# Reordering the third slot and the router's gate steps in a fused attention and mixture-of-experts kernel

## What the kernel computes

```
x = x + conv_attention(layernorm over channels(x))
    k, q = relu(1x1 conv), v = 1x1 conv           # 64 channels, 8 heads
    context = sum over pixels of k v^T, per head
    out = 1x1 conv(context^T q)
t = x as rows of 64 channels, one row per pixel
t = t + moe(layernorm(t))
    probs = softmax(t @ router_w + router_b)      # 8 experts
    the two largest are kept and rescaled to sum 1
    out = sum over the two of prob * (t @ expert_w[e] + expert_b[e])
```

## Time and profile before

| | us |
|---|---|
| median of 3 runs | 676.02 |
| the profiled execution, whole | 671.9 |
| its span, first to last instruction | 670.1 |
| PE busy | 616.2 |
| DVE busy | 515.1 |
| ACT busy | 425.2 |
| POOL busy | 396.1 |

### The profile page before, as it was taken

How to read it: one execution, slowest core, us unless ns; L and a number is a source line. 1 busy time by engine, 2 the same in 40 slices (tenths; PEclk the granted TensorE clock), 3 DMA queues, 4 the chain that set the end, 5 groups by cost and what they waited for, 6 DMA issues and landing times.

```text
span 670.1 us, 21498 instructions
## 1 busy us (share of the span) xinstructions
PE 616.2 (92%) x8318; PEld 276.3 (41%) x8318; DVE 515.1 (77%) x1176; ACT 425.2 (63%) x832; POOL 396.1 (59%) x350
## 2 busy tenths in 40 slices
PE   3799989779999999999999999999999999998887
PEld 1566656444444444444444444444332332332222
DVE  3534455978888888889788787987799999989844
ACT  2355545576666675766757576766766776766642
POOL 7232342237565655666666556655577777777875
PEclk9799989999999999999999999999999999999999
DMA  6223635666555566655545665554565667446542
GB/s 149 56 76 79 146 97 129 150 167 159 122 122 134 126 147 146 159 142 138 133 111 130 147 152 127 129 116 104 133 154 127 157 172 170 101 111 142 126 111 48
DMA packets 32662, 86.21 MB, mean 129 GB/s; under 512 B 7650, under 2 KB 7826, under 8 KB 32562
## 3 DMA queue, kind: packets, MB, share of 16 engines
q1 hardware_dynamic: 32082, 84.64, 52.8%
q0 software_dynamic: 288, 0.19, 0.2%
q10 hardware_dynamic: 192, 0.01, 0.0%
HBM read 34.47 MB, written 16.78 MB: 76 GB/s over the span
## 4 chain that ended last, share of the span: by engine, by line
PE 62%; DVE 18%; ACT 10%; issue 7%; DMA 1%; POOL 1%; ACTq 0%; DVEq 0%; SPq 0%; POOLq 0%
PE bank L1092 26%; PE bank L1078 7%; PE bank L1015 5%; PE bank L993 4%; PE bank L979 4%; DVE z L826 3%; PE bank L938 3%; PE bank L1089 3%; PE bank L962 3%; DVE x L731 3%; ACT grows L569 2%; DVE xnT L686 2%; PE bank L1039 2%; DVE osb L836 2%; ACT L529 2%
## 5 line engine op out<-in xcount | busy, mean ns | idle before, releaser
L442 POOL TENSOR_TENSOR z<-gbs,x1d 128x512 f32<-128x512 f32 x256 | 320.2, 1275 | 185.2 <-ACT gbs L575 72.6
L1095 PE MATMUL bank<-z,ew 128*64 128x512 f32 x512 | 243.7, 598 | 0.0
L1092 PE MATMUL bank<-z,ew 128*64 128x512 f32 x512 | 243.6, 598 | 0.0
L826 DVE TENSOR_TENSOR z<-bank,x1d 128x512 f32<-128x512 f32 x256 | 164.7, 675 | 16.2 <-PE bank L1078 16.2
L575 ACT COPY gbs<-bank 128x512 f32<-128x512 f32 x256 | 140.7, 594 | 43.8 <-PE bank L1078 41.3
L433 POOL TENSOR_TENSOR xsq<-xin 128x512 f32<-128x512 f32 x64 | 65.4, 1043 | 81.7 <-DMA xin<-in_x_dram 76.0
L1078 PE MATMUL bank<-grows,sel 64*64 64x512 f16 x1024 | 93.2, 387 | 16.3 <-ACT grows L569 7.3
L1092 PEld LDWEIGHTS bank<-z,ew 128*64 128x64 f32 x512 | 64.9, 136 | 104.6 <-issue 96.3
L503 ACT COPY xn<-bank 128x512 f32<-128x512 f32 x64 | 34.4, 589 | 62.8 <-PE bank L938 62.8
L1095 PEld LDWEIGHTS bank<-z,ew 128*64 128x64 f32 x512 | 64.7, 136 | 0.0
L686 DVE TENSOR_TENSOR xnT<-bank,rstd 128x512 f32<-128x512 f32 x64 | 41.0, 682 | 30.2 <-PE bank L924 28.5
(11 more groups left out here) (135 smaller groups left out, 804.8 us busy)
## 6 DMA issues: line engine op xcount, KB each, us to landing
x1d<-x SPq DMA_DIRECT2D x128, 256.0 KB, 4.5
xin<-in_x_dram SPq DMA_DIRECT2D x64, 256.0 KB, 4.2
x_again<-in_x_dram SPq DMA_DIRECT2D x64, 256.0 KB, 4.2
out_dram<-osb SPq DMA_DIRECT2D x128, 128.0 KB, 2.4
k<-in_const_dram SPq DMA_DIRECT2D x1, 453.5 KB, 3.8
ew_nat<-in_L_ffn_expert_w_dram POOLq DMA_DIRECT2D x2, 64.0 KB, 6.4
sel<-in_const_sel_dram SPq DMA_DIRECT2D x1, 128.0 KB, 3.4
bk_rows<-bk_wide ACTq DMA_DIRECT2D x6, 1.0 KB, 1.7
```

What stands on the lines that cost most here:

```text
L442: pool.tensor_tensor(z[:, 1, i % R_Z, :], gbs[:, i % R_Z, :], x1d[:, g % 2, 1, u * NT:(u + 1) * NT], ALU.mult).then_inc(z_pool, 1)
L826: dve.tensor_tensor(z[:, 0, i % R_Z, :], bank[:, :], x1d[:, g % 2, 0, u * NT:(u + 1) * NT], ALU.mult).then_inc(taken_of(("spread", i, 0)), 1)
L1092: pe.matmul(out_bank[0:C, :], ew[:, j, :], z[:, 0, i % R_Z, :], start=False, stop=(j == PAIRS - 1), skip_group_check=True).then_inc(prod_d ...
L1095: pe.matmul(out_bank[C:P, :], ew[:, j, :], z[:, 1, i % R_Z, :], start=False, stop=(j == PAIRS - 1), skip_group_check=True).then_inc(prod_d ...
```

## The change

Five edits are made together.

1. **Third slot.** The first iteration's spreading comes ahead of the queries, on PE, in the rotation of banks, and on ACT (`copy_gates` ahead of `take_queries`).
2. **Root of x's deviations.** ACT's `root_x` moves from the end of the second slot to the end of the third.
3. **Exponents.** The exponent over all logits moves to the first fourth slot (phase 2), and waits only for gate step 11. The exponent of the second choice becomes `second_exponent`, in the second slot of the odd step (phase 4).
4. **Gate steps.** The 27 steps are cut otherwise: (0,4), (4,9) with (9,11) behind x's deviations, (11,13), (13,16), (16,18), (18,21) with (21,24) behind x's deviations, (24,26), (26,27). The first part of each fourth slot stands ahead of x's deviations.
5. **Squares of x1.** `square_x1` is one ACT instruction of 1024 columns, not two of 512.

The core of the diff:

```
@@ bank_uses; likewise in the lists of ACT and PE
             if k == 2:
+                for i in iterations(n, k + 1)[:1]:
+                    yield from (("spread", i, s) for s in range(S))
                 if real(n - L_KEYS):
                     yield from (("queries", n - L_KEYS, s) for s in range(S))
-                for i in iterations(n, k + 1)[:1]:
-                    yield from (("spread", i, s) for s in range(S))
@@ ACT
-            def square_x1(g, u):
+            def square_x1(g):
...
-                nc.scalar.activation(x1sq[:, u * NT:(u + 1) * NT], x1[:, g % R_X1, u * NT:(u + 1) * NT], ACT.Square
-                                     ).then_inc(x1_squared, 1)
+                nc.scalar.activation(x1sq[:, :], x1[:, g % R_X1, :], ACT.Square).then_inc(x1_squared, 1)
             def exponent(p):
+                act.wait_ge(gate_dve, p * N_GATE + 11)
+                nc.scalar.activation(gex[:, :, :], g_own, ACT.Exp).then_inc(exp_done, 1)
+
+            def second_exponent(p):
                 act.wait_ge(gate_dve, p * N_GATE + 16)
-                nc.scalar.activation(gex[:, :, :], g_own, ACT.Exp).then_inc(exp_done, 1)
                 nc.scalar.activation(gstat[:, 4, :], gstat[:, 2, :], ACT.Exp).then_inc(exp_done, 1)
-            gate_steps = {1: root_dev, 5: exponent, 7: high, 8: low}
+            gate_steps = {1: root_dev, 2: exponent, 4: second_exponent, 7: high, 8: low}
-                    if k == 1 and real(n - L_COLS):
-                        root_x(n - L_COLS)
                     if k == 3:
                         if real(n - L_ATTEND):
-                            for u in range(U):
-                                square_x1(n - L_ATTEND, u)
+                            square_x1(n - L_ATTEND)
+                    if k == 2 and real(n - L_COLS):
+                        root_x(n - L_COLS)
@@ DVE
+                def tied_first():
+                    dve.wait_ge(exp_done, p * 2 + 1)
+                    return tied(g_own)()
...
+                    for phase, (k0, k1) in gates_by_phase.items():
+                        if quad_in(n, k, phase) is not None:
+                            gates(quad_in(n, k, phase), k0, k1)
                     if k == 3 and real(n - L_COLS):
                         x_deviations(n - L_COLS, 4, N_XSTAT)
-                    for phase, (k0, k1) in gates_by_phase.items():
+                    for phase, (k0, k1) in gates_behind.items():
                         if quad_in(n, k, phase) is not None:
                             gates(quad_in(n, k, phase), k0, k1)
```

More of the change, by code:

```diff
@@ L529, in root_x @@
                 nc.scalar.activation(xstat[:, 4, :], xstat[:, 3, :], ACT.Sqrt).then_inc(xstat_root, 1)
-            def square_x1(g, u):
-                when_taken(act, ("attended", g, u))
+            def square_x1(g):
+                for u in range(U):
+                    when_taken(act, ("attended", g, u))
                 if g:
                     when_filled(act, ("rows", g - 1 + L_ROUTE, 0))
-                nc.scalar.activation(x1sq[:, u * NT:(u + 1) * NT], x1[:, g % R_X1, u * NT:(u + 1) * NT], ACT.Square
-                                     ).then_inc(x1_squared, 1)
+                nc.scalar.activation(x1sq[:, :], x1[:, g % R_X1, :], ACT.Square).then_inc(x1_squared, 1)
             def root_dev(p):
@@ L619, in _ @@
                     if k == 2:
+                        for i in iterations(n, k + 1)[:1]:
+                            copy_gates(i)
                         if real(n - L_KEYS):
@@ L622, in _ @@
                                 take_queries(n - L_KEYS, s)
-                        for i in iterations(n, k + 1)[:1]:
-                            copy_gates(i)
                     for i in iterations(n, k + 1)[1 if k == 2 else 0:]:
                         copy_gates(i)
-                    if k == 1 and real(n - L_COLS):
-                        root_x(n - L_COLS)
                     if k == 3:
                         if real(n - L_ATTEND):
-                            for u in range(U):
-                                square_x1(n - L_ATTEND, u)
+                            square_x1(n - L_ATTEND)
+                    if k == 2 and real(n - L_COLS):
+                        root_x(n - L_COLS)
                     for phase, step in gate_steps.items():
@@ L778, in less, with total @@
                     return lambda: dve.tensor_tensor(values, values, over_experts(gstat[:, k, :]), ALU.subtract)
-                def less_second():
+                def tied_first():
+                    dve.wait_ge(exp_done, p * 2 + 1)
+                    return tied(g_own)()
+                def total():
                     dve.wait_ge(exp_done, p * 2 + 2)
-                    return less(g_all, 2)()
+                    return dve.tensor_scalar(second_work, gstat[:, 4, :], 1.0, None, ALU.add)
                 dev = newton(bstat[:, 0, :], bstat[:, 3, :], bstat[:, 1, :], dev_work)
@@ L795, in gates @@
                     less(g_own, 0),
-                    tied(g_own), most(g_all, 1), mask(gk[:, :, :]),
+                    tied_first, most(g_all, 1), mask(gk[:, :, :]),
                     lambda: dve.scalar_tensor_tensor(g_all, gk[:, :, :], -BIG, g_own, ALU.mult, ALU.add),
                     most(g_all, 2),
-                    less_second,
+                    less(g_all, 2),
                     tied(g_all), most(g_all, 1), mask(g_all),
                     lambda: dve.tensor_tensor(g_all, g_all, gk[:, :, :], ALU.add),
-                    lambda: dve.tensor_scalar(second_work, gstat[:, 4, :], 1.0, None, ALU.add),
+                    total,
                     lambda: dve.reciprocal(gstat[:, 3, :], second_work),
@@ L1144, in _ @@
                     if k == 2:
+                        for i in iterations(n, k + 1)[:1]:
+                            broadcast(i)
                         if real(n - L_KEYS):
                             make_queries(n - L_KEYS)
-                        for i in iterations(n, k + 1)[:1]:
-                            broadcast(i)
                         if real(n - L_ATTEND):
```

5 lines of the change are left out of this document (3 added, 2 removed).

## The result

| | before | changed |
|---|---|---|
| median of 4 runs, us | 675.46 (672.19 to 676.94) | 666.47 (664.89 to 667.36) |
| profiled execution, us | 671.9 | 666.57 |
| its span, us | 670.1 | 664.8 |

The ratio is 0.9886 with the interval 0.9857 to 0.9915: 1.1% faster. 662 was forecast, in a range from 655 to 671. The sign is right and the time lies in the range, but of a forecast gain of 13.9 us the medians show 9.0, so about a third is missing. The two profiled executions differ by only 5.3 us. I therefore compare stretches, from one column transpose (the start of L1036, which was L1025) to another.

What follows compares the result with a forecast made beforehand. PE was taken to set the full stage's pace, DVE close behind in the late stage. Terms -14.9 - 2.0 - 1.0 + 4.0 = -13.9 took 671.9 to 658.0; moved up 4.1 to the median, 662 us, range 655 to 671.

Steps and rivals of the forecast that it cites:

- third slot, root moved: Full stage, third slot: PE's second spreading no longer waits for ACT's queries; -14.9 us, bounds -12.1 and -16.4.
- gate steps and deviations on DVE: Fourth slots: x's deviations, behind gate steps, no longer wait for POOL, so xnT comes sooner; -2.0 us, bounds 0 and -2.6.
- exponent in the even fourth slot: Even fourth slot: ACT gets +1.56 us of load and exponent, mostly covered by idle time; costed at nothing.
- ramp: Steps 14 and 16: -1.4 us of PE's wait for the low gates, +0.4 of ACT waiting for DVE; sum -1.0.
- late stage: Steps 35 to 44: no slack covers the exponent's table load; +0.8 us in each of five pairs, +4.0, bounds 0 and +8.
- The rival that rested on the drain: Even step's end: ACT's load reaches PE, by drain or an earlier bank request; 5 to 8 us more, 669 us; chance 0.15 with smaller mixtures.
- What is left of DVE's gain is covered by PE: Fourth slots: beyond the -2.0 us taken for an earlier xnT, DVE's gain brings nothing more.
- rival (d): Even fourth slot: deviations meet POOL's next pair, gate step 11 comes late, holding ACT at the exponent; 688 us, chance 0.09.
- Gate step 11 late: Even fourth slot: the eleventh gate step ends over 1.3 us after ACT's load, delaying lg, keys, gate copies and POOL's products.
- stay above 18.8: Sign against the prediction: even steps of the full stage stay above 18.8 us, where 17.9 to 18.2 was forecast.
- The second spreading waits for DVE over 0.5 us: Sign against the prediction, third slot: PE's second spreading waits for DVE over 0.5 us.
- ACT idle over 0.5 us between the load and the exponent: Sign against the prediction: ACT stands idle over 0.5 us between the table load and the exponent.

Runs made afterwards that it cites:

- pair 0 late: The changed kernel with exponents, gate steps and deviations of the first pair of groups (steps 14 to 16) placed as in the kernel before; 666.3 us, ratio 0.9885.
- the run with late exponents: The changed kernel with exponents, gate steps and deviations of the last six pairs (steps 34 to 46) placed as in the kernel before; 663.62 us, ratio 0.9852.

## Why the prediction was right, and by how much not

Terms as forecast, against the two profiled executions:

| term | forecast | measured | by what |
|---|---|---|---|
| third slot, root moved | -14.9 (-12.1 to -16.4) | -16.0 | L1050 to L1100 over the 18 steps: 37.2 to 21.2 us |
| gate steps and deviations on DVE | -2.0 (-2.6 to 0) | +5.8 | rest of steps 17 to 34 |
| exponent in the even fourth slot | 0 | within the line above | |
| ramp | -1.0 | +1.4 | steps 11 to 16 |
| late stage | +4.0 (0 to +8) | +2.2 | steps 35 to 43 |
| start and end | 0 | +1.3 | chance of the start +1.5, tail -0.2 |
| sum | -13.9 | -5.3 | spans, 670.1 to 664.8 (terms rounded) |

**What held.** *Third slot, with the root moved* was right in mechanism and size: the wait is gone in all 18 steps. It is all that was there. Two numbers of the term were off: the 0.15 us that I left for the odd steps didn't reach PE (1.5 us in all), and steps 18 and 26 had 2.41 us from L1039 to L1089 before, not the 2.65 of step 24, so that the 16.4 were 0.4 too many. No drain appears around the early table load either; the changed kernel's ACT at step 24:

```profile
293.65 1.28 ACT L547 ACT_TABLE_LOAD   x1
294.95 0.38 ACT L547 ACTIVATE gex<-bank 128x256 f32<-128x256 f32 x1
```

The exponent starts 0.02 us after the load. The rival that rested on the drain didn't come.

**What failed.** The step is *Gate steps and deviations on DVE*, down to its last sentence, "What is left of DVE's gain is covered by PE". It was worked out from where the deviations would land in POOL's 3.01 us of pause in the earlier trace rows. Three things were overlooked. First, the kernel before had a meeting in the even fourth slot too: x's L652 took 1.29 us in step 24, which the earlier trace rows don't show, and waited POOL's product out for all that stood behind it. With gate steps ahead, one of them took over that wait, and x's steps came late enough to meet the next pair. Second, a gate step of the five that now stand ahead of them, the gates' own Newton step, has two inputs in SBUF as x's have; I charged it "at most 0.43", and it took 1.16. Only the deviations were treated as exposed to POOL. Third, the pause was taken as fixed. It shrank step by step with the waits that were removed: 3.01 us before, 2.49 with the new third slot alone (253.73 less the end at 251.24), 1.64 with the root moved as well, 1.67 in the changed kernel. The timelines of POOL with the new third slot alone, then with the root moved as well, even fourth slot:

```profile
248.74 2.50 POOL L442 TENSOR_TENSOR z<-gbs,x1d 128x512 f32<-128x512 f32 x2
253.73 2.52 POOL L442 TENSOR_TENSOR z<-gbs,x1d 128x512 f32<-128x512 f32 x2 [2.49 <-issue]
```

```profile
257.07 2.51 POOL L442 TENSOR_TENSOR z<-gbs,x1d 128x512 f32<-128x512 f32 x2 [1.64 <-issue]
```

Together they put x's third step 0.11 us behind the start of POOL's pair. PE paid with 0.83 us at the even step's end, and the next first slot grew from 2.08 to 2.73 us between L1036 and the bias matmul, since result and xnT came late as well. Of the 2.25 us that this pair gained (0.47 and 1.47 in the third slots, 0.31 in the even step's first slot, where xnT was waited for), 0.89 + 0.65 = 1.54 went back (0.89 with the start of L1036, of which 0.83 is the marked wait). Five of the eight pairs paid so: 5 x 1.54 = 7.7 against 8 x 0.31 = 2.5 gained makes +5.2, near the +5.8 of the table. That is the first half of rival (d), two instructions that meet POOL, at a third of its price. "Gate step 11 late" wasn't what carried it to PE; it was DVE's products. I gave it 0.09 as a whole and nothing of it in the forecast, though by its own numbers the deviations came near to POOL's pair. (Its sum has a slip: 662 + 25 is 687, not 688.)

The rule of the Trainium skill that I cited, "SBUF — State Buffer", "Who interferes with whom", was right and applied to too few instructions. The run with one operand in PSUM shows both halves of it: 1.16 us with two SBUF inputs, 0.20 with one, POOL being at work in both.

That the time lay in the range has therefore some luck in it: the third slot gave 1.1 us more than forecast and the late stage cost 1.8 less, against 7.8 lost on DVE and 2.4 in the ramp. By the profiled executions alone the time would be 666.57 + 4.1 = 670.7, at the very edge of the range.

*Ramp*: the mechanism named for step 14's keys (ACT waits for DVE at the exponent) was there, priced at 0.4 us, and cost 3.1 in its step; it was returned in the next two but for 0.9 us. In step 16 PE's wait for the gates fell from 3.27 to 1.30 us and the step from 14.50 to 12.65, but that is not the -1.4 forecast: with the root moved and nothing else of the rest the step took 13.95 us, and in the changed kernel with pair 0 late 14.53. What releases these steps in turn stays open.

*Late stage*: the mechanism held and was over-sized. Pairs took 27.36 us (27.01 before), +0.35 for +0.8, below the 27.5 that I had set as a lower edge. Over the stretch it was 2.2 us, of which the run with late exponents took back 2.0.

All three signs that had been named as making the prediction wrong appeared, if only just. Even steps that "stay above 18.8": the even step was 18.83, and it pointed at just this fault. The second spreading waits for DVE over 0.5 us: its weight loads did, by 0.52 to 0.73 us in six odd steps, but beside matmuls, so that L1050 to L1100 stayed at 1.17 us (1.22 in step 17). ACT idle over 0.5 us between the load and the exponent: once, 0.98 us, for step 15's keys. Odd and even steps were to take 17.9 to 18.2 us and took 18.59 and 18.83.

**What stays open.** The medians differ by 9.0 us and the profiles by 5.3. The start accounts for 1.6 of that (93.13 and 94.76 us up to step 12); the rest is within what single executions scatter, and wasn't taken apart. Why the ramp's steps give back what step 15 loses, and why the ramp is 1.6 us or more longer wherever pair 1 has the early places, wasn't followed to its end. A kernel with the changed cuts and the late exponent was not tried, so the two have no price of their own. Nor was the single square run by itself.

## What to carry to other kernels

When small VectorE instructions are moved, look at each one's operands before its length: here a 128x16 instruction with both inputs in SBUF took 0.17 or 1.2 us depending on whether POOL had started, and a second copy of one operand in PSUM, 0.18 us on ScalarE, was worth 6.5 us over 17 steps. A pause of another engine that a forecast puts work into must be worked out anew after the change, since removing a wait moves it. And a change of several parts is best run part by part: the third slot's order and the moved root alone took 4 us less behind step 12 than the whole change. Compare stretches between fixed points of the program, since here the start alone scattered by 6 us.

## What the runs showed of the hardware that I hadn't expected

A meeting of VectorE with POOL costs at most the rest of one POOL product, not of the pair: in the rows shown the delayed instruction took 1.14 to 1.29 us (1.34 was the longest in steps 17 to 34 of all the kernels), where POOL's pair took 2.50 to 2.52. It can hit again at once, though: in the kernel with the deviations last, two instructions in a row took 1.14 and 1.19 us, one product each. And PE's clock fell with one wait of 3.52 us: 0.58 was granted over the 5 us behind it, and the group of 32 sums took 2.03 us for 1.15, while the kernel before, with 1.53 of 4 us busy in the corresponding stretch, stayed at 1.00. Its two windows:

```profile
119.00:123.00 4.00, 1.53 (x45) 1.37 (x43) 3.76 (x12) 1.14 (x4) 0.15 (x1) 1.00 0.21 50
123.00:128.00 5.00, 5.00 (x114) 2.57 (x113) 4.45 (x15) 4.07 (x9) 0.18 (x1) 1.00 0.41 110
```
